# A first phase written in another order: 16-bit K features with the norm as a bias, weight pieces fetched a step ahead, zeroing begun in the prologue

## What is computed

```python
xn = _layernorm(x, axis=-1)
x = x + _L0_gnn_ref(xn, edge_index, ...) + _L0_mix_ref(xn[None], ...)[0]
x = x + _L0_ffn_ref(_layernorm(x, axis=-1)[None], ...)[0]
...
def _phi(t, random_features):
    norm_sq = 0.5 * jnp.sum(t * t, axis=-1, keepdims=True)
    proj = jnp.einsum('bhnd,md->bhnm', t, random_features)
    return jnp.exp(proj - norm_sq) * (1.0 / math.sqrt(M))
...
q_p = _phi(q, random_features)
k_p = _phi(k, random_features)
kv = jnp.einsum('bhnm,bhnd->bhmd', k_p, v)
out = jnp.einsum('bhnm,bhmd->bhnd', q_p, kv)
k_sum = jnp.sum(k_p, axis=2)
```

## Time and profile before

| | us |
|---|---|
| median of 3 runs | 2603.47 |
| the profiled execution | 2589.16 |
| its span (first to last instruction) | 2587.0 |
| mean granted TensorE clock | 0.972 of full |

### The profile page before, as it was taken

The page is one execution under the profiler, slowest core; times in us unless marked ns, Lnnn a source line. Parts: engine busy times, 40 slices in busy tenths (PEclk is TensorE's granted clock), DMA queues, the critical chain, the costliest instruction groups (busy, mean ns, idle before and its releaser), DMA issues.

```text
span 2587.0 us, 44622 instructions
## 1 busy us (share of the span) xinstructions
PE 2388.9 (92%) x16483; PEld 1621.4 (63%) x16483; DVE 1331.4 (51%) x2865; ACT 803.8 (31%) x1093; POOL 802.6 (31%) x563
## 2 busy tenths in 40 slices
PE   5999899899999999998899999999998899999576
PEld 3777677687766666665565566666664556666365
DVE  7646566574566766766313444454441334444444
ACT  3323233342374654745112222222220001110033
POOL 0000121223677877777572000000000000000165
PEclk9999899899999999999999999999998999999799
DMA  6798979554413133231517999999986654444286
GB/s 238 274 364 300 390 253 392 181 169 116 97 1 62 1 61 56 5 62 1 135 1 199 293 284 313 286 274 291 281 278 236 201 203 168 169 160 159 74 171 129
DMA packets 192194, 474.17 MB, mean 183 GB/s; under 512 B 74864, under 2 KB 81882, under 8 KB 182460
## 3 DMA queue, kind: packets, MB, share of 16 engines
q1 hardware_dynamic: 109996, 381.82, 40.7%
q0 software_dynamic: 71264, 61.03, 17.8%
q10 hardware_dynamic: 10800, 29.50, 2.9%
HBM read 266.99 MB, written 210.77 MB: 185 GB/s over the span
## 4 chain that ended last, share of the span: by engine, by line
PE 53%; DMA 15%; issue 11%; POOL 10%; DVE 6%; ACT 2%; SPq 2%; POOLq 0%; DVEq 0%; ACTq 0%
PE pair L1794 30%; PE pair L372 13%; POOL cells L706 10%; DMA cells<-arena 8%; PE pair L1619 2%; DMA arena<-in_g_t 2%; DVE arena L1164 2%; PE pair L1567 2%; PE pair L1630 2%; PE pair L1938 1%; PE pair L1925 1%; DMA arena<-in_w_qkv 1%; DMA arena<-in_ffn_in 1%; DMA arena<-ahl_dram 1%; DMA arena<-cells 1%
## 5 line engine op out<-in xcount | busy, mean ns | idle before, releaser
L372 PE MATMUL pair<-arena 128*128 128x384 f16 (+2 forms) x5760 | 906.6, 319 | 26.4 <-SPq L361 8.1
L706 POOL DMA_INDIRECT cells<-arena x392 | 638.5, 1629 | 718.5 <-DMA cells<-arena 576.4
L1794 PE MATMUL pair<-arena 128*128 128x384 f16 x4900 | 820.9, 328 | 28.3 <-SPq L361 11.0
L372 PEld LDWEIGHTS pair<-arena 128*128 128x128 f16 (+1 forms) x5760 | 566.9, 99 | 351.5 <-issue 29.1
L1794 PEld LDWEIGHTS pair<-arena 128*128 128x128 f16 x4900 | 475.9, 98 | 338.9 <-issue 18.2
L1619 PE MATMUL pair<-arena 128*128 128x256 f32 x600 | 167.2, 412 | 17.5 <-ACT arena L812 17.5
L736 POOL DMA_INDIRECT slots<-arena x25 | 28.8, 1153 | 492.2 <-DVEq L1493 459.6
L1630 PEld LDWEIGHTS pair<-arena 128*128 128x128 f32 x1200 | 158.1, 198 | 10.0 <-ACT arena L837 4.5
L1630 PE MATMUL pair<-arena 128*128 128x66 f32 x1200 | 156.4, 279 | 3.6 <-ACT arena L837 3.6
L837 ACT ACTIVATE arena<-pair 128x512 f32<-128x512 f32 x150 | 88.5, 592 | 197.9 <-PE pair L1619 197.6
L1725 PE MATMUL pair<-arena 128*128 128x320 f32 x480 | 134.5, 433 | 0.0
(11 more groups left out here) (194 smaller groups left out, 2288.3 us busy)
## 6 DMA issues: line engine op xcount, KB each, us to landing
cells<-arena SPq DMA_DIRECT2D x50, 1600.0 KB, 14.6
arena<-cells SPq DMA_DIRECT2D x25, 1600.0 KB, 9.8
arena<-cells POOLq DMA_DIRECT2D x25, 1600.0 KB, 13.1
ahl_dram<-arena SPq DMA_DIRECT2D x25, 1600.0 KB, 13.7
arena<-ahl_dram SPq DMA_DIRECT2D x25, 1600.0 KB, 7.8
arena<-in_x SPq DMA_DIRECT2D x70, 384.0 KB, 4.4
arena<-key_dram SPq DMA_DIRECT2D x28, 896.0 KB, 5.9
split_w<-arena SPq DMA_DIRECT2D x32, 384.0 KB, 6.3
```

The costliest lines, as they stand in the source:

```text
L372: ins = nc.tensor.matmul(dst[half], left(k, a), right(k, b, half), start=start and n == 0, stop=stop and n == 2)
L706: nc.gpsimd.indirect_dma_start(cells[k], bass.IndirectOffsetOnAxis(ap=idx_all[:, m:m + 1], axis=0), val_all[:, m:m + 1], None, bounds_chec ...
L1794: ins = nc.tensor.matmul(pair[u][:, half, 0:HD], a[:, 0, s * P:(s + 1) * P], X[part][:, s, half * HD:(half + 1) * HD], start=(s == 0 and p ...
```

## The change

All of it is in phase 1 and its prologue.

1. **K features**: ACT casts the two heads of K to 16 bits (`cast_k`, two copies of 64x640) and squares all 128 rows into `ksq`. DVE writes the remainders K - high into the other 64 rows (`low_k`). PE multiplies [high, low] with 16-bit `rf_hi` and `rf_lo`: four 16-bit matmuls of 256 columns for a tile, where there were two float32 ones. The norm is made apart: `k_norms`, five float32 matmuls of 2 columns for a pair, into unused columns of the K bank. ACT copies them (`norms_k`), and exp takes them as its bias, one exp of 256 columns for each head. The split of `rf` moves from the start of phase 2 to the prologue.
2. **Order**: `k_up(c, 0)` comes before the last V tile. `k_norms(p+1)` stands before the last `k_sums` of unit p. The copy of the low transposed half (`evict_lo`) goes from DVE to ACT. DVE does `mark` ahead of the K remainders, and `inverse` (the end of the statistics) later.
3. **Weight pieces**: ACT and DVE handle the piece that was asked for one slot earlier. SP does its step last in a unit, and in a chunk's head after the loads of rows.
4. **Ones column** of `vals`: written in chunk 0 and the last chunk alone.
5. **Zeroing**: ten of the 50 DMAs go into the prologue, two after each of the first five row stores; then three in each unit until all are issued (unit 13, where it was unit 17). BOTH is 1. ACT waits for the store of the edge keys before it writes its first buffer. `degrees` uses 64 rows x 50 columns in place of 128 x 26.

```diff
-BOTH = 4
-CLEAR_CHUNKS = 3
+BOTH = 1
+CLEAR_FIRST, CLEAR_STEP = 10, 3
...
+            sp.wait_ge(consts, 2)
             for n in range(TC):
                 store_xn(n)
+                clear(CLEAR_FIRST * n // TC, CLEAR_FIRST // TC)
...
-                    presplit_step(presplit_slot(c, 2 + p))
-                    if c < CLEAR_CHUNKS:
-                        for i in range(2 * T * m // (CLEAR_CHUNKS * PAIRS), 2 * T * (m + 1) // (CLEAR_CHUNKS * PAIRS)):
-                            clear_tile(sp, i // T, i % T).then_inc(cleared[i // T], 16)
+                    clear(CLEAR_FIRST + CLEAR_STEP * m, CLEAR_STEP)
...
+                    presplit_step(presplit_slot(c, 2 + p))
...
+            def cast_k(c, p):
+                s, j = slot_use[("k", p)]
+                act.wait_ge(slot_full[s], c * uses[s] + j + 1)
+                for h in range(2):
+                    rows = slice(h * DH, (h + 1) * DH)
+                    nc.scalar.copy(halves_of(kh[p % 2][rows, h, :]), bank_pair(s)[rows])
+                nc.scalar.activation(halves_of(ksq[p % 2]), bank_pair(s), ACT.Square).then_inc(k_cast, 1)
...
             act.wait_ge(vals_clear, 1)
+            act.wait_ge(key_stored, 16)
...
+                    norms_k(c, p)
                     for t in range(TC):
...
-                        nc.scalar.activation(kp_sb[q], bank(4 + q), ACT.Exp).then_inc(kp_exp, 1)
+                        for h in range(2):
+                            ins = nc.scalar.activation(kp_sb[q][:, h * M:(h + 1) * M], bank(4 + q)[:, h * M:(h + 1) * M],
+                                                       ACT.Exp, bias=knorm[:, p % 2, 2 * t + h:2 * t + h + 1])
+                        ins.then_inc(kp_exp, 1)
...
-                        if t == 2 and p + 1 < PAIRS:
-                            square_k(c, p + 1)
-                    presplit_hi(act, presplit_slot(c, 2 + p))
+                        if t == 1 and p + 1 < PAIRS:
+                            cast_k(c, p + 1)
+                        if more and t == 3 and p:
+                            evict_lo((c + 1) * TC + p - 1)
+                    presplit_hi(act, presplit_slot(c, 2 + p) - 1)
...
-            def copy_k(c, p):
+            def low_k(c, p):
...
+                dve.wait_ge(k_cast, c * PAIRS + p + 1)
...
                 for h in range(2):
-                    ins = nc.tensor.matmul(bank(4 + n % 2)[:, h * M:(h + 1) * M],
-                                           kk[p % 2][:, h, t * P:(t + 1) * P], (rfa, rfb)[h], start=True, stop=True)
+                    for m, weights in enumerate((rf_hi, rf_lo)):
+                        ins = nc.tensor.matmul(bank(4 + n % 2)[:, h * M:(h + 1) * M],
+                                               kh[p % 2][:, h, t * P:(t + 1) * P], weights,
+                                               start=(h == 0 and m == 0), stop=(m == 1), skip_group_check=True)
...
+            def k_norms(c, p):
+                s, j = slot_use[("k", p)]
+                pe.wait_ge(k_low, 2 * (c * PAIRS + p) + 2)
+                for t in range(TC):
+                    ins = nc.tensor.matmul(pair[s][:, 0, HW + 2 * t:HW + 2 * t + 2], ksq[p % 2][:, t * P:(t + 1) * P],
+                                           minus_half, start=(t == 0), stop=True, skip_group_check=True)
+                ins.then_inc(k_norm, 1)
```

189 lines of the change are left out of this document (100 added, 89 removed).

## The result

| | before | after |
|---|---|---|
| median, 8 runs each | 2602.04 (2596.18 to 2614.09) | 2582.08 (2579.61 to 2591.46) |
| the profiled execution | 2589.16 | 2581.01 |
| phase 2 starts at | 696.66 | 687.40 |
| last scatter starts at | 1372.80 | 1293.40 |
| graph round starts at | 1405.68 | 1398.55 |

The ratio is 0.9927, 95% interval 0.9904 to 0.9949. The sign is as forecast and the time lies in the forecast range, but the likeliest value was twice too generous. The two profiled executions differ by 8 us only, the medians by 20: that is the first thing to explain. The graph round starts 7 us earlier than before, where 43 were forecast.

The account below looks back on a forecast made before the run. Bound: phase 1 on PE and, beside it, the scatters, ending within a few us of each other. Phase 1: 660.4 - 40 - 27 + 12 - 10.8 - 4.4 + 28 = 618, 43 less; against 2603.47 that predicts 2560 us, range 2520 to 2595.

Parts of the forecast that it names:

- (d): Weight pieces: look-ahead saves 10.8 us in chunk 3 and 4.4 in chunk 2, nothing in chunks 0 and 1.
- (e): Prologue: key store waits behind ten zeroings, so PE stands 25 us, plus 3 at lower clock: +28 us.
- (c): New waits in a unit: PE stands about 0.4 us for exp behind K's casts, 30 times: +12 us.
- (f): Ones column, `mark` first, smaller `degrees`, and `evict_lo` on ACT: all hidden beside PE, at no cost.
- (g): Scatters end near 1230 us, about 100 us of slack, so nothing holds back phase 1's gain.
- Rival 4: The scatters still end last, ahead of the graph round: no gain, 2600 us; chance 0.04.
- (a): PE work of a unit: 16-bit features and separate norms save 1.34 us a unit, 40 us over 30 units.
- (b): Chunk head: the 3.5 us wait and some 2 us of lower clock go, five times: 27 us saved.
- the second: Rival: DMA and prologue make the first two chunks end 20 us later still, 2580 to 2595 us; chance 0.20.
- The first: Rival: in the units, `k_norms` waiting for `low_k` makes the K path the bound, up to 2620 us; chance 0.08.

Follow-up runs that it names:

- b_both1: The kernel before with BOTH = 1 in place of 4, one number changed; ratio 0.9943.
- b_same: The kernel before, unchanged, profiled a second time; 2612.93 us.
- b_both1_ahead: The kernel before with BOTH = 1 and the look-ahead of the weight pieces, old K features kept; ratio to before 0.9959.
- a_late: The changed kernel with its ten early zeroings moved behind the first loads, to the start of chunk 0; ratio to before 0.9918.
- a_front_shift_deg: a_spread with weight pieces one slot earlier, old edge counts, and 22, 15 and 13 zeroings in chunks 0, 1, 2; ratio to before 0.9820.
- a_spread: The changed kernel with the old spread of zeroings (50 over 18 units, none in the prologue), BOTH = 1 kept; ratio to before 0.9827.
- a_old_zero: The changed kernel with the old spread of zeroings and BOTH = 4; ratio to before 0.9968.

## Why the prediction was half right

In the profile the graph round starts at 1398.55, 36 us later than forecast (1405.68 less 42.7). The chunks are 29 of it: 21 in chunks 0 and 1, which (d) and (e) put too low, and 8 in chunks 3 and 4, mostly (c) and (f). The end of the phase, which is in no term, adds 4.6 us of wait (5.50 for 0.91) and 2 of lower clock; the graph round's own wait is 2 us shorter, and some 2 us are not accounted for. The forecast median missed by 22 only, because the step from the profile to the median failed the other way.

**The sum against the median failed, by 13 us in my favour.** I took 43 us off a median that lay 14 above the profile, as if that distance would stay. With the wait for the scatters off (b_both1) the kernel before gains 15 us, so most of that distance was this wait, short in the profile (5.24) and 25.94 in b_same, and my own (g) took the scatters off the path. The changed kernel's median lies 1 us above its profile (2582.08, 2581.01). Carried through, the forecast would have been 2546 + 1, and the miss 35 us. That the time lies in my range is partly luck. Rival 4 (scatters end last) described the kernel before, which I had read as "both paths end within a few us of each other".

**(a)** holds: features 0.109 us a matmul, norms 0.22, 1.31 us less a unit (1.34).

**(c)** was mis-sized: 0.65 us a unit in place of 0.4. Two exps of 256 columns take 0.84 us for a tile, where I had 0.77; the sentence on the Trainium skill ("ScalarE: Activation LUTs", What ACT_TABLE_LOAD costs; 93 ns more for each per-partition operand) gave 0.95. The trace shows 473 ns for one, 83 above my slope, which bears the 93 out, but two in a row take 0.84 and not 0.95, so the second overlaps the first. The exp is 0.07 of the 0.25 that were missing, and the second late start in a unit, which the sum didn't have, 0.11.

**(f)** failed in one point. "A smaller `degrees`" is larger for PE: 50 columns for 26, 0.55 for 0.35 us, 14 matmuls 30 times, 6 us. I had costed it on DVE alone. With `k_sums` behind the norms (+0.18) and (c) (+0.25) that is 0.6 us, against the 0.5 by which a unit misses, and 3 of the 4 us in chunks 3 and 4.

**(b)** holds in its place: the head has no such wait. The number, 27 forecast and 29 measured by undoing it (0.0110, with some 8 us of uncertainty), agrees partly by chance: I priced the old waits for squares (3.5 us each), and what comes up without the new head is a wait for the new remainders (27.7 us in six). That the new head is also a condition for the gain of the rest, I had not seen.

**(d)** failed twice. *Chunk 1*, 143 for 130: "plus some 10 us of the head in which little is asked for". In stretches of 10 us, chunk 1 of the changed kernel:

```profile
213.65:223.65 10.00, 7.09 (x38) 4.03 (x36) 3.89 (x9) 2.42 (x3) 3.08 (x2) 0.85 0.48 152
223.65:233.65 10.00, 10.00 (x70) 6.78 (x68) 5.52 (x12) 4.51 (x7) 1.64 (x1) 0.98 0.78 230
233.65:243.65 10.00, 9.63 (x80) 7.72 (x80) 9.33 (x41) 7.87 (x15) 3.78 (x2) 1.00 0.49 136
...
283.65:293.65 10.00, 6.85 (x65) 6.55 (x64) 8.93 (x36) 7.34 (x14) 1.58 (x1) 1.00 1.05 405
```

For 30 us the engines carry 173 GB/s on average. Against 405 that is 7 MB, 17 us; the chunk moved 49.8 MB (123 us at 405), and 123 + 17 = 140 of 143.2. The zeroings wait in SP's list for the first unit (they are issued at 240.91) while the queue is half empty. *The look-ahead*: I valued part 3 at 15 us. No run gives its worth: it brings nothing on the kernel before (b_both1_ahead), and undone in the changed one, with the head's order left new, it costs 44 (or 28 with the early zeroing). I had looked at waits inside the units alone; the runs show them at the head.

**(e)** had the right wait (26.1 for 25) in the right place and the wrong meaning: a_late removes it for nothing. What is paid is some ten more zeroings in chunk 0, whose DMA share goes from 0.75 to 0.87. The term was also too small. Two stretches of the changed kernel's chunk 0:

```profile
95.00:105.00 10.00, 10.00 (x73) 7.08 (x72) 7.62 (x39) 6.10 (x12) 0.00 (x0) 1.00 0.01 2
175.00:185.00 10.00, 10.00 (x59) 9.39 (x58) 2.28 (x5) 3.27 (x7) 0.00 (x0) 0.50 1.02 389
```

The gap in the DMA engines' work was not filled, as (e) counts on, but moved from 70 to 80 us to 85 to 105: SP issues the next zeroings only at 104.75, again behind the first unit's key load. And PE is busy 129.25 us with 960 matmuls that take 114.86 in chunk 3: 14 us more, at a mean granted clock of 0.84 for 0.99, where (e) had 3 for the lower clock. PE's waits in the chunk, 26.1 us and 3.5 others, are fewer than (e)'s 25 and the 11 that stayed lost by (d).

**(g)** holds: 1293 for 1230, slack about 70 for 100 us. From 1200 us on 39 scatters took 93 us, in which the forecast rate makes 45. That BOTH = 1 was behind it, and not the early zeroing, only the runs showed.

**The end of the phase** was missing: 5.5 us, and 2 us of lower clock. The last chunk takes 112 us and not 108, which I had named as a sign of being wrong.

Of the rivals, the second (DMA and prologue eat it, 2580 to 2595) gave the measured time and the right place, chunks 0 and 1, 21 us later than forecast. The time is luck in part: it starts from the same 2560, and the 13 us too many in that are made up by chunks 3 and 4 and the phase's end. The first (K path bound) did not occur: `k_norms` waited for `low_k` 0.8 us in all.

Still open: why PE stays at the lower clock long after a wait (from 313.65 to 323.65 us it is busy 10.00 of 10 us at a granted clock of 0.53; its last wait, 4.88 us, ended at 305.98), and why chunk 0 pays as much for a zeroing as the full chunks do although its DMA share is 0.82 (a_front_shift_deg).

## What to carry to other kernels

Two paths that end within a few us of each other make the time vary, and a gain on one alone may not show: profile the kernel twice before you take a difference off its median, and price a change on each path alone. When a queue is shared, put the steps that wait for an engine behind the ones that wait for nothing, and count a bulk transfer by its bytes in the stretch where it falls, not by the wait that it shows up as. Look-ahead can move a wait to the next place that has no other work, as here to the head of a chunk; see what that is before you count the gain.

## What the runs showed of the hardware that I had not expected

- A float32 matmul of 2 columns costs 0.22 us (five in 1.09), as much as one of 66 columns (four in 0.84 us).
- Once the queue is full, issuing DMAs is itself slow: SP takes 10 to 11 us to issue three zeroings late in chunk 1 of the changed kernel, and 2.41 us for three at 240.91, where the engines move 136 GB/s (233.65 to 243.65). Everything behind them in its list starts that much later.
- With one chain the scatters of the kernel before start 4 to 10 us apart from 272 to 550 us, and two chains give nearly twice the rate beside a queue as busy (15 to 8 in 50 us, a_spread and a_old_zero, at DMA shares of 0.65 and 0.57).
